# Two of three convolutions go from F(2,3) to F(4,3) along the row, and the attention of the next band starts one step earlier

## What is computed

```
stk = _neighborhood(x)                      # 3x3 shifted views, zero padded
q = einsum('bhwd,de->bhwe', x, Q_P)
k = einsum('bhwkd,de->bhwke', stk, K_P)
v = einsum('bhwkd,de->bhwke', stk, V_P)
alpha = softmax(einsum('bhwke,bhwe->bhwk', k, q) * mask)
t = x + einsum('bhwk,bhwke->bhwe', alpha, v)
t_in = t
t = relu(conv(t, ff1_kernel) + ff1_bias)
t = relu(conv(t, ff2_kernel) + ff2_bias)
t = relu(conv(t, ff3_kernel) + ff3_bias)
return t_in + t
```

## Time and profile before

| | |
|---|---|
| time, median of 3 runs (lowest to highest) | 2644.49 us (2639.14 to 2647.08) |
| time of the profiled execution | 2641.18 us |
| its span, first to last instruction | 2639.0 us |
| busy: PE, PEld | 2451.5 us (93%), 1300.4 us (49%) |
| busy: DVE, ACT, POOL | 1892.5 us (72%), 1183.0 us (45%), 15.4 us (1%) |
| DMA | 311.68 MB, 40.6% of 16 engines' span |
| granted TensorE clock | 0.978 of 2.4 GHz |

### The profile page before, as it was taken

One profiled execution on the slowest core, in us unless ns is written; L12 is line 12 of the kernel. 1 busy time (PEld: TensorE's weight loads), 2 busy tenths in 40 slices (PEclk: granted clock), 3 DMA queues, 4 the chain that ended last, 5 costly groups with the idle time before them and its releaser, 6 DMA issues.

```text
span 2639.0 us, 54500 instructions
## 1 busy us (share of the span) xinstructions
PE 2451.5 (93%) x19992; PEld 1300.4 (49%) x19992; DVE 1892.5 (72%) x2767; ACT 1183.0 (45%) x3171; POOL 15.4 (1%) x23
## 2 busy tenths in 40 slices
PE   5999999998899999999889999999988999999997
PEld 3545554554455555545354555455445554554543
DVE  4777777775577777777667777777756777777775
ACT  2544444543454444444344444444435444544433
POOL 2000000000000000000000000000000000000000
PEclk7999999999899999999989999999999999999999
DMA  4433443443344434433244344344423443444343
GB/s 117 134 117 114 121 132 107 124 129 99 98 128 126 132 100 118 140 115 116 87 135 120 109 121 134 112 119 126 133 78 118 122 133 107 123 129 124 107 121 99
DMA packets 217442, 311.68 MB, mean 118 GB/s; under 512 B 15460, under 2 KB 149412, under 8 KB 210724
## 3 DMA queue, kind: packets, MB, share of 16 engines
q1 hardware_dynamic: 217324, 310.12, 40.6%
HBM read 135.47 MB, written 33.82 MB: 64 GB/s over the span
## 4 chain that ended last, share of the span: by engine, by line
PE 71%; DVE 15%; issue 8%; ACT 4%; DVEq 1%; DMA 0%; SPq 0%; ACTq 0%
PE conv_banks L430 26%; PE conv_banks L444 18%; PE conv_banks L407 9%; DVE work L736 6%; PE conv_banks L411 4%; DVE dtl L714 3%; PE mix_bank L384 3%; PE score_banks L369 3%; PE mix_bank L395 3%; ACT dth L606 3%; PE score_banks L358 2%; DVE tf L685 2%; DVE work L698 2%; PE score_banks L350 1%; PE score_banks L366 1%
## 5 line engine op out<-in xcount | busy, mean ns | idle before, releaser
L444 PE MATMUL conv_banks<-du,w2f 64*128 64x512 f32 (+2 forms) x3264 | 745.9, 588 | 57.6 <-DVE work L736 49.0
L430 PE MATMUL conv_banks<-dodd,w3f 128*64 128x512 f32 (+1 forms) x1656 | 499.0, 577 | 10.8 <-DVE dodd L698 10.8
L430 PE MATMUL conv_banks<-deven,w3f 128*64 128x512 f32 (+1 forms) x1656 | 492.0, 567 | 4.2 <-DVE deven L698 3.7
L444 PEld LDWEIGHTS conv_banks<-du,w2f 64*128 64x128 f32 x3264 | 294.7, 190 | 377.6 <-issue 256.4
L533 ACT ACTIVATE prob<-score_banks,negmax 128x100 f32<-128x100 f32 x1040 | 344.9, 360 | 177.8 <-DVE negmax L665 177.8
L726 DVE TENSOR_TENSOR work<-conv_banks,m_sb 128x512 f32<-128x512 f32 (+3 forms) x273 | 179.7, 658 | 327.3 <-PE conv_banks L444 262.6
L736 DVE TENSOR_TENSOR work<-conv_banks,work 128x1024 f32<-128x1024 f32 (+3 forms) x273 | 312.3, 1165 | 60.2 <-PE conv_banks L430 40.6
L563 ACT COPY m_sb<-conv_banks 128x512 f32<-128x512 f32 (+3 forms) x273 | 146.9, 564 | 376.4 <-PE conv_banks L430 165.1
L606 ACT CAST dth<-work 128x1024 fp32r<-128x1024 f32 x130 | 136.1, 1047 | 303.0 <-DVE work L698 302.0
L430 PEld LDWEIGHTS conv_banks<-deven,w3f 128*64 128x64 f32 x1656 | 171.8, 137 | 155.0 <-issue 109.3
L430 PEld LDWEIGHTS conv_banks<-dodd,w3f 128*64 128x64 f32 x1656 | 149.0, 136 | 189.5 <-issue 148.8
(11 more groups left out here) (82 smaller groups left out, 2719.3 us busy)
## 6 DMA issues: line engine op xcount, KB each, us to landing
xk<-x_keys SPq DMA_DIRECT2D x66, 800.0 KB
xc<-x_bands SPq DMA_DIRECT2D x67, 650.0 KB, 5.5
dodd<-dodd SPq DMA_DIRECT2D x68, 512.0 KB, 2.9
xr<-x_bands SPq DMA_DIRECT2D x264, 128.0 KB, 4.8
kept<-tf SPq DMA_DIRECT2D x129, 256.0 KB, 5.0
out<-work SPq DMA_DIRECT2D x60, 512.0 KB, 2.6
dth<-dth SPq DMA_DIRECT2D x68, 256.0 KB, 2.3
dtl<-dtl SPq DMA_DIRECT2D x68, 256.0 KB, 2.4
```

The costliest lines, as they stand in the source:

```text
L430: return nc.tensor.matmul(bank[rows, lo * 128:hi * 128], w3f[:, m, s, odd * C:odd * C + C], source[:, lo + s // 2:hi + s // 2, m], start=s ...
L444: return nc.tensor.matmul(conv_banks[:, bank_of(which, j), lo * 128:hi * 128], w2f[rows, STREAMS[j], 2 * (which == EVEN) + s], du[rows, lo ...
```

## The change

The first and second convolution become F(4,3): four output columns from six transformed inputs, which are made from every fourth column. `weights4` makes the weights once, in ten VectorE instructions for each of the two convolutions. A bank now holds two streams of 256 columns, so the first convolution has three "pairs" of streams in place of four tiles with three products each, and it is plain float32: `t_high` and `t_low` are gone. The third convolution stays F(2,3).

The input transform is now `differences` (four instructions that read every fourth column of `tf` or `relued`) and `outer4`, `far4`, `near4` (five instructions on their results). The output transform is `u_middle`, four times `u_four`, and `u_outer` for the first convolution, and `y_middle`, four times `y_four`, and `y_outer` for the second. ScalarE's ReLU, `relu4`, writes every fourth column.

`ahead` names the next band. Its `r_product` and the first half of its `scores`, `max_scores`, `exps` and `scale` are done at the end of the step before, and a step begins with `turn(b, 0)`. `r_product` writes to the banks of the scores. `scale` stays on VectorE. `add_x` becomes one instruction for both images.

```
+def conv1_pair(G, k, b, j):
+    if j == 0:
+        pe.wait_ge(y_mid, before(G))
+        pe.wait_ge(dt_done, b * 5)
+        pe.wait_ge(t_kept, G * 16 + 16)
+    elif j == 2:
+        pe.wait_ge(y_out, before(G))
...
+    for m in range(2):
+        for n, s, lo, hi in taps:
+            last = nc.tensor.matmul(bank[:, m * 256 + lo * 64:m * 256 + hi * 64], w1f[:, 2 * j + m, n],
+                                    dt[:, 2 * j + m, lo + s:hi + s],
...
 def begin2(G, k, j):
...
+    for m in range(2):
+        for s in range(2):
+            even = tap2(k, EVEN, j, m, LOWER, s, m == 0 and s == 0, False)
+            odd = tap2(k, ODD, j, m, UPPER, s, m == 0 and s == 0, False)
+    even.then_inc(half_done, 1)
+    odd.then_inc(half_done, 1)
 def end2(G, k, j):
+    pe.wait_ge(half_done, G * 6 + (2 * j + 2))
+    for m in range(2):
+        odd = tap2(k, ODD, j, m, LOWER, 1, False, m == 1)
+        even = tap2(k, EVEN, j, m, UPPER, 0, False, m == 1)
```

ScalarE's ReLU and VectorE's new transforms:

```
+def relu4(to, rows, src, lo, hi, shift):
+    return nc.scalar.activation(
+        to[rows, lo:hi, :, 1:1 + W].rearrange("c s i (w n) -> c n s i w", n=4),
+        src[rows, :, lo * 64:hi * 64].rearrange("c n (s i w) -> c n s i w", i=2, w=WT4),
+        ACT.Relu, bias=shift)
...
+def columns(src, slots, *at):
+    if len(at) == 1:
+        return src[:, 0:slots, :, at[0]:at[0] + W - 3:4]
+    first = at[0] - (at[1] - at[0] == 1)
+    view = src[:, 0:slots, :, first:first + W].rearrange("c s i (w m) -> c m s i w", m=4)
+    return view[:, 1:3] if first < at[0] else view[:, 0:4:3]
+def differences(src, slots, done):
+    p = parts_sb[:, :, 0:slots]
+    nc.vector.tensor_tensor(p[:, 1:3], columns(src, slots, 3, 4), columns(src, slots, 1, 2),
+                            ALU.subtract).then_inc(done, 1)
+    nc.vector.tensor_tensor(p[:, 0:4:3], columns(src, slots, 2, 5), columns(src, slots, 0, 3),
+                            ALU.subtract).then_inc(done, 1)
+    for n in range(2):
+        nc.vector.scalar_tensor_tensor(p[:, 4 + n], columns(src, slots, 1 + n), -4.0,
+                                       columns(src, slots, 3 + n), ALU.mult, ALU.add).then_inc(done, 1)
```

The step of ScalarE after the change, which sets what its two ReLUs of the second convolution stand in front of:

```
 def step(G, k, b, q, par, att):
+    nxt = ahead(k, b, q, par)
+    if att:
+        keep_turned(b, 0)
+    keep_u2(G, k)
     if k:
         relu_conv2(G, k - 1, ODD, 1)
         relu_conv2(G, k - 1, EVEN, 1)
     if att:
         exps(b, 2)
         exps(b, 3)
+    keep_o2(G, k)
     relu_conv1(G, k)
     if att:
         keep_y(b, 0)
+        keep_turned(b, 1)
     relu_conv3(G, k)
     if att:
         keep_y(b, 1)
+    if nxt:
+        keep_r(nxt[0], 0)
+        keep_r(nxt[0], 1)
+        exps(nxt[0], 0)
+    keep_y2(G, k, ODD)
+    keep_y2(G, k, EVEN)
+    if nxt:
+        exps(nxt[0], 1)
```

And that of VectorE:

```
+    if k:
+        y_four(G, k - 1, 0, 1)
+        y_four(G, k - 1, 3, 1)
+        y_four(G, k - 1, 2, 1)
+        y_outer(G, k - 1, 1)
+        y_four(G, k - 1, 1, 1)
+    if att:
+        max_scores(b, 2)
+        max_scores(b, 3)
     if k:
         inputs(G, k - 1, ODD, 0, 1)
+        inputs(G, k - 1, EVEN, 0, 1)
+    u_middle(G, k)
+    u_four(G, k, 0)
+    u_four(G, k, 3)
+    if att:
+        scale(b, 2)
+    u_outer(G, k)
+    u_four(G, k, 1)
+    u_four(G, k, 2)
     if k:
         inputs(G, k - 1, ODD, 1, 1)
+        inputs(G, k - 1, EVEN, 1, 1)
+    if att:
+        scale(b, 3)
+    u_differences(G, k)
+    o_middle(G, k)
+    u_inputs(G, k)
+    o_outer(G, k)
     finish(G, k, b)
+    if att:
+        add_x(k, b, par)
+        t_differences(b, par)
+    if nxt:
+        max_scores(nxt[0], 0)
+        max_scores(nxt[0], 1)
+    if att:
+        t_inputs(G, b)
+    if nxt:
+        scale(nxt[0], 0)
+    y_middle(G, k)
+    if nxt:
+        scale(nxt[0], 1)
```

More of the change, by code:

```diff
@@ L62, in pairs3 @@
     return (2, RP) if k == 1 else (0, 2) if k == 0 else (0, RP)
[L65 to L66 removed]
 def new_slots(which, k):
[L71 removed]
+    return {ODD: 1, EVEN: 2}[which] if k == BANDS else RP
 def build(nc, x_bands, x_keys, qt2, kt, vbd, w1, w2, w3, b1, b2, b3, window, eye, eye16, out):
@@ L473, in _ @@
             pe.wait_ge(xc_in[0], 16)
-            for half in range(2):
-                r_product(0, 0, half)
+            r_product(0, 0, 0)
+            r_product(0, 0, 1)
             scores(0, 0, 0)
@@ L482, in _ @@
             v_product(0)
+            pe.wait_ge(probt_ready, 2)
+            pe.wait_ge(xc_in[1], 16)
+            r_product(1, 1, 0)
+            r_product(1, 1, 1)
+            scores(1, 1, 0)
             pe.wait_ge(w_ready, 3)
@@ new lines, in near4, with t_differences, t_inputs @@
+            def near4(to, slots, done):
+                p = parts_sb[:, :, 0:slots]
+                for m, op in ((2, ALU.add), (0, ALU.subtract)):
+                    nc.vector.tensor_tensor(to[:, m, 1:1 + slots], p[:, 5], p[:, 4], op).then_inc(done, 1)
+            def t_differences(b, par):
+                dve.wait_ge(t_ready, b + 1)
+                differences(tf[:, par], RP, t_parts)
+            def t_inputs(G, b):
+                dve.wait_ge(t_parts, b * 4 + 4)
+                if G is not None:
+                    dve.wait_ge(t_kept, G * 16 + 32)
+                outer4(dt, RP, dt_done)
+                far4(dt, RP, dt_done)
+                near4(dt, RP, dt_done)
@@ new lines, in u_four, with u_outer @@
+            def u_four(G, k, n):
+                lo, hi = pairs1(k)
+                at = slice(lo * 64, hi * 64)
+                dve.wait_ge(u_mid, this(G))
+                if n == 0 and k:
+                    dve.wait_ge(y_relued[EVEN], G)
+                four(lambda h: u_sums[:, h, at], lambda h: u_even[:, h, at], lambda h: u_odd[:, h, at], n, u_summed)
+            def u_outer(G, k):
+                lo, hi = pairs1(k)
+                at = slice(lo * 64, hi * 64)
+                dve.wait_ge(tile_done, filled(G, CONV1, 2))
+                dve.wait_ge(u_summed, G * 4 + 2)
+                bank = conv_banks[:, BANK1[2]].rearrange("c (h n) -> c h n", h=2)
+                o = u_sums[:, 0:4:3, at]
+                nc.vector.tensor_tensor(o, bank[:, :, at], o, ALU.add).then_inc(u_out, 1)
@@ new lines, in y_four, with y_outer @@
+            def y_four(G, k, n, behind=0):
+                lo, hi = pairs2(k)
+                at = slice(lo * 64, hi * 64)
+                dve.wait_ge(y_mid, this(G, behind))
+                if n == 0:
+                    dve.wait_ge(u_relued, G + (1 - behind))
+                four(lambda h: y_sums[:, :, h, at], lambda h: y_even[:, :, h, at], lambda h: y_odd[:, :, h, at],
+                     n, y_summed)
+            def y_outer(G, k, behind=0):
+                lo, hi = pairs2(k)
+                at = slice(lo * 64, hi * 64)
+                dve.wait_ge(tile_done, G * FILLS + (fill_of(EVEN, 2) + 1 - FILLS * behind))
+                dve.wait_ge(y_summed, G * 4 + (2 - 4 * behind))
+                banks = conv_banks[:, BANK2[2]:BANK2[2] + 2].rearrange("c o (h n) -> c o h n", h=2)
+                o = y_sums[:, :, 0:4:3, at]
+                nc.vector.tensor_tensor(o, banks[:, :, :, at], o, ALU.add).then_inc(y_out, 1)
@@ L738, in inputs, with o_outer @@
+            def o_outer(G, k):
+                lo, hi = pairs3(k)
+                m03 = conv_banks[:, 2:4, lo * 128:hi * 128]
+                both = sums3[:, lo:hi].rearrange("c s i (w n) -> c n (s i w)", n=2)
+                dve.wait_ge(tile_done, filled(G, CONV3, 3))
+                dve.wait_ge(o_mid, this(G))
+                nc.vector.tensor_tensor(both, m03, both, ALU.add).then_inc(o_out, 1)
             def inputs(G, k, which, part, behind=0):
                 if part == 0:
-                    dve.wait_ge(relu_done, relus(G, which, behind))
@@ L826, in _ @@
             schedule(dve, step)
-            middle(ALL_STEPS, 0, CONV3)
-            outer(ALL_STEPS, 0, CONV3)
+            o_middle(ALL_STEPS, 0)
+            o_outer(ALL_STEPS, 0)
             finish(ALL_STEPS, 0, PAIRS * BANDS + 1)
```

537 lines of the change are left out of this document (248 added, 289 removed).

## The result

The changed kernel takes 2725.68 us (median of 4 runs, 2723.6 to 2728.3) against 2643.05 of the kernel before on the same chip: ratio 1.0313, 95% interval 1.0294 to 1.0332. Slower, as forecast, but by 83 us and not by 22. The profiled execution has a span of 2721.7 us and a mean granted clock of 0.956.

The account below looks back on a forecast made before the run. TensorE was taken to set the step now, a loop through TensorE and VectorE after the change. 4 x (14 x 1.12 - 10.9) + 3 = +22 us on 2641.2 gave 2663, as median 2666 us; range 2550 to 2740.

Parts of the forecast that it names:

- The weight loads: TensorE's two 128-column loads per 0.225 us slot were claimed to fit; rival that they show: 2880 us, chance 0.04.
- the slots of 256 columns: TensorE's float32 convolution matmuls after the change: 0.225 us a slot, 36 slots or 8.1 us in the second convolution.
- The stride's price: Every-fourth-column access in differences and relu4: 0.8 ns an element, 1.23 us more a differences call, 0.82 a ReLU.
- The rule that I had drawn, two neighbours served at once: Strided access: every element at stride four is a break, while stride two costs nothing because two neighbours are served together.
- The walk through the step: Middle step timed from turn(b, 0) through TensorE, VectorE and ScalarE's ReLUs: next turn at 39.41 us, 1.1 more than now.
- the middle step's term: Middle steps, k = 1 to 14 of four pairs: each 1.12 us longer, entering the sum as 4 x 14 x 1.12.
- has 3.6 us of slots left: Step's end, scores to last scale: 7.3 us in which TensorE has only 3.6 us of slots left.
- the end steps' term: Pair ends, k = 15, 16 and 0: about 33, 33 and 31 us, 97.5 against 108.4, 10.9 less each pair.
- start and end: Kernel's start and end: 3 us more, estimated, for longer weight transforms and the transform behind them.
- A stride of four costs nothing: Rival on strided differences and ReLUs: no extra cost, step 37.7 us, end steps 94.4, total 2556 us; chance 0.25.
- The loop doesn't bind: Rival on the middle step: VectorE works ahead, TensorE's 34.0 us a step stand, total 2340 us; chance 0.07.
- Twice the elements: Rival on stride-four access: costs twice the elements or more, step 39.9 us, ends 99, total 2699 us; chance 0.18.

Follow-up runs that it names:

- after: The changed kernel as described, run beside the kernel before: 2725.68 us, ratio 1.0313.
- 1: Changed kernel with the two differences instructions walking columns so that neighbours are read and stored in pairs, outer4 as two instructions: 2691.69 us.
- 3: Changed kernel with relu4 as two instructions that write neighbours in pairs, sums stored to match, u_outer and y_outer two instructions each: 2649.74 us.
- 5: Changed kernel with both the differences and the ReLUs walking columns in neighbouring pairs: 2613.43 us.
- experiment 4: Changed kernel plus two unused float32 matmuls of 512 columns on TensorE ahead of the second convolution's last tile: 2702.73 us.
- 6: Changed kernel reordered: V product before second convolution, attention inputs before maxima, scalings behind its middle, ScalarE's copy before exponentials; no work removed: 2631.83 us.
- experiment 8: Changed kernel with four of the five VectorE instructions of u_inputs left out, output not the reference's: 2724.49 us.
- 2: Changed kernel with ScalarE's copy for the second convolution (keep_y2, twice) ahead of the next band's first exponentials: 2775.6 us.
- 10: Changed kernel with V product, attention inputs and scalings reordered on TensorE and VectorE only, ScalarE's exponentials still ahead of its copy: 2782.15 us.
- 11: Changed kernel with only the attention's five transform instructions moved ahead of the next band's maxima on VectorE: 2896.62 us.

## Why the prediction was right in direction and wrong in size

**Right.** The weight loads don't show, and the slots of 256 columns take 0.23 us (2.79 for 24 records, two to a slot). The stride's price, the number that no row had, was right: 0.8 ns an element on VectorE (runs after and 1). For a ReLU 1.97 was assumed and 2.04 measured. There is luck in it: the price was carried over from a row of TensorE to two other engines, and no run shows that the three have one cause. The rule that I had drawn, two neighbours served at once, agrees with experiments 1, 3 and 5. The Trainium skill (Vector Engine (DVE) Microarchitecture Reference, section Measured stream behaviour on trn2) says that between runs of two or more adjacent words that start on an 8-byte boundary any hop is free; VectorE's rows in pairs agree as to the neighbours, with 0.61 us for 512 elements, and on which boundary the runs start no row shows. The walk through the step held on VectorE, counted from the turn at 1035.72:

| | walk | after |
|---|---|---|
| `v_product` starts | 26.89 | 26.92 |
| `add_x` starts | 28.50 | 28.32 |
| `t_differences` ends | 32.80 | 32.65 |
| maxima end | 33.76 | 33.61 |
| `scale(nxt, 0)` ends | 36.37 | 36.25 |
| `y_middle` ends | 38.65 | 38.52 |
| last `scale` ends | 39.34 | 39.21 |
| next `turn` starts | 39.41 | 40.29 |

This step begins with a late turn, so VectorE is ahead of TensorE at its head, and ScalarE's ReLUs start 3.28 us after the turn. The walk has 3.50. In experiment 4, where the turn waits for VectorE as in the walk, they start after 3.75, and a step is 39.6 us.

**Wrong, the middle step's term (+25 us of the miss of 61).** The failing step is the sentence that TensorE "has 3.6 us of slots left" in the 7.3 us between scores and scale, so that the turn hangs on VectorE alone. I had not walked ScalarE there. Its copy for the second convolution stands behind `exps(nxt, 0)`, which stand behind the maxima; TensorE waits 2.5 us for it. The wait alone would have fitted: 3.6 + 2.5 is below 7.3. What doesn't fit is that the granted clock falls behind it, and the last 24 records take 4.6 us; at the full clock they take 3.2 behind such a wait (at 569.05, and in experiment 4). Experiment 4, with that clock held, has 1.26 us a step where the walk said 1.12 (7 us in all; the rows above point to the head of the step); the other 0.34 us is the clock (18 us in all). The Trainium skill (TensorE: Matmul & The Clock Gate, section HAM oscillation) describes this pattern, a wait that comes back in each turn of a loop and takes the clock down each time. Its waits are for a DMA and last some 3 to 5 us; here the wait is for ScalarE and lasts 2.5, the windows above show 0.63 over the tile, and the clock falls in 36 of 52 steps, not in each.

**Wrong, the end steps' term (+19 us).** From k = 14 to the next k = 1 I forecast 136.9 us (97.5 and a middle step) and 143.2 is measured. I called it "the same walk with the narrower tiles" and did not do it step by step. TensorE's timeline there shows what such a walk leaves out, waits for the same copy:

```profile
680.45 3.23 PE L442 MATMUL conv_banks<-du,w2f 64*128 64x256 f32 x24 [2.12 <-ACT work L574]
...
690.86 2.82 PE L428 MATMUL conv_banks<-dodd,w3f 128*64 128x512 f32 x5 [1.75 <-DVE dodd L707]
716.10 3.19 PE L442 MATMUL conv_banks<-du,w2f 64*128 64x64 f32 x24 [3.62 <-ACT work L574]
721.95 0.37 PE L362 MATMUL score_banks<-eye_sb 64*128 64x2 f32 x1 [2.66 <-issue]
...
753.92 1.50 PE L442 MATMUL conv_banks<-du,w2f 64*128 64x192 f32 x13 [3.15 <-ACT work L574]
```

The walks in pairs take 5.9 us off this stretch (137.3 in experiment 5), the order alone 2.2 (141.0 in 6). How the rest divides among its waits no run separates. A wait for the copy need not cost its length: behind the one of 3.62 us the turn waits another 2.66 us, for something that the profile does not name.

**Wrong, start and end (+16 us).** I had +3 for both and let the end steps' gain count at the last pair too; they cost +9.7. Which of the prologue's parts (weight transforms, the second band's maxima ahead of the first) makes the 6 us up to k = 1 was not tried.

**The rivals.** "A stride of four costs nothing" had 2556 us: experiment 5, which makes it nearly true by another walk, has 2613, so even there the sum was 57 us short; its end steps (99.0 us, with a middle step of 38.3 taken off 137.3) are 4.6 us a pair above the 94.4 of that rival. "The loop doesn't bind" (2340 us) is refuted by the time and by TensorE's 86%; that VectorE's total sets the step instead is refuted by experiment 8, and a loop is shown by 2, 6, 10 and 11, which remove no work and move the time by +50, -94, +56 and +171 us. "Twice the elements" came nearest in time (2699) with the wrong reason. That the scaling stays on VectorE had no experiment of its own.

## What to carry to other kernels

When the slowest path runs through several in-order queues, walk every queue in it, the engine that looks idle (ScalarE, 45%) first: what it does second may be what TensorE needs first. Judge a move of an instruction together with the moves on the other engines; here two sets of moves that cost 50 and 56 us alone gain 94 together. And walk a float32 stride of four in pairs of neighbours before giving up on a transform that needs it: that was worth 112 us here.
